# Spreading a block's row maxima one step later in the TensorE stream of an attention kernel

## The reference, cut to what matters

```python
x = _layernorm(x + _L0_attn_ref(x, Wq, Wk, Wv, Wo))
x = _layernorm(x + _L0_xattn_ref(x, ctx_768, ...))
x = _layernorm(x + _L0_ffn_ref(x, ...))

# cross-attention: 8 heads of 128, 1792 queries, 6000 keys
sim = jnp.einsum('hid,hjd->hij', qh, kh) * SCALE
mean = jnp.mean(sim, axis=-1, keepdims=True)
sim = (sim - mean) * ATTN_MATRIX_SCALE + mean
attn = jax.nn.softmax(sim, axis=-1)
out = jnp.einsum('hij,hjd->hid', attn, vh)
```

## Time and profile before

| what | before |
|---|---|
| median of 3 runs | 2277.97 us (2276.93 to 2280.52) |
| profiled execution | 2285.66 us, its span 2283.5 us |
| PE busy | 2233.7 us, 98% |
| DVE, ACT, POOL busy | 83%, 82%, 83% |
| granted TensorE clock | 0.996 over the span |
| chain that ended last | PE 76%, POOL 11%, DVE 5%, ACT 3%, DMA 3%, issue 2% |
| the 56 blocks | maxima reduced at 185.1 to 2152.7 us of the span |

### The profile page before, as it was taken

How to read it: one execution, slowest core, us unless ns; L and a number is a source line. 1 busy time by engine, 2 the same in 40 slices (tenths; PEclk the granted TensorE clock), 3 DMA queues, 4 the chain that set the end, 5 groups by cost and what they waited for, 6 DMA issues and landing times.

```text
span 2283.5 us, 61997 instructions
## 1 busy us (share of the span) xinstructions
PE 2233.7 (98%) x25966; PEld 1967.6 (86%) x25966; DVE 1891.8 (83%) x2111; ACT 1865.6 (82%) x2231; POOL 1899.2 (83%) x1157
## 2 busy tenths in 40 slices
PE   8999999999999999999999999999999999999998
PEld 4468998899889998999888997999889988988886
DVE  6878888888888888888888888888888888888877
ACT  5357888888888888888888888888888888888855
POOL 8865988888888897888888897888888888899853
PEclk9999999999999999999999999999999999999999
DMA  8310000000000000000000000000000000010320
GB/s 241 121 52 6 9 8 18 9 9 9 16 9 9 11 9 16 8 9 11 16 9 9 9 18 6 11 9 8 16 9 11 9 8 9 8 32 29 96 79 33
DMA packets 65302, 57.80 MB, mean 25 GB/s; under 512 B 32768, under 2 KB 57856, under 8 KB 65024
## 3 DMA queue, kind: packets, MB, share of 16 engines
q1 hardware_dynamic: 65024, 53.81, 8.3%
HBM read 30.99 MB, written 15.47 MB: 20 GB/s over the span
## 4 chain that ended last, share of the span: by engine, by line
PE 76%; POOL 11%; DVE 5%; ACT 3%; DMA 3%; issue 2%; SPq 0%; POOLq 0%; DVEq 0%; ACTq 0%
PE psum L460 30%; PE psum L492 10%; PE psum L485 10%; POOL e_lo L1720 7%; PE psum L488 5%; PE psum L490 5%; PE psum L625 4%; PE psum L615 4%; DVE run_max L1165 2%; POOL e_hi L1714 2%; ACT ring L917 2%; PE psum L763 2%; DMA fold_t<-run_max 1%; PE psum L632 1%; PE psum L811 1%
## 5 line engine op out<-in xcount | busy, mean ns | idle before, releaser
L1720 POOL TENSOR_TENSOR e_lo<-ring,e_hi 128x1024 f16<-128x1024 f32 (+1 forms) x665 | 1388.2, 2103 | 193.2 <-ACT ring L932 165.4
L917 ACT ACTIVATE ring<-psum 128x1024 f32<-128x1024 f32 (+1 forms) x672 | 674.5, 1004 | 169.4 <-POOL e_lo L1720 84.7
L1185 DVE SCALAR_TENSOR_TENSOR ring<-ring,psum 128x1024 f32<-128x1024 f32 (+1 forms) x672 | 793.0, 1187 | 0.4 <-PE psum L729 0.4
L1165 DVE TENSOR_TENSOR run_max<-psum,run_max 128x1024 f16<-128x1024 f32 (+1 forms) x560 | 670.2, 1197 | 146.0 <-ACT ring L917 142.3
L460 PE MATMUL psum<-qx_hi,k_hi 128*128 128x256 f16 x2632 | 718.4, 273 | 9.8 <-DVE run_max L1165 9.7
L460 PE MATMUL psum<-qx_hi,k_lo 128*128 128x256 f16 x2632 | 718.0, 273 | 0.0
L460 PE MATMUL psum<-qx_lo,k_hi 128*128 128x256 f16 x2632 | 717.9, 273 | 0.0
L492 PE MATMUL psum<-v_main,e_lo 128*128 128x129 f16 x4032 | 704.2, 220 | 0.0
L932 ACT ACTIVATE ring<-ring 128x1024 f32<-128x1024 f32 (+1 forms) x672 | 696.3, 1037 | 0.6
L485 PE MATMUL psum<-v_main,e_hi 128*128 128x257 f16 x2016 | 550.7, 273 | 1.6 <-POOL e_lo L1720 1.6
L488 PE MATMUL psum<-v_main,e_hi 128*128 128x129 f16 x2016 | 443.6, 220 | 0.0
(11 more groups left out here) (205 smaller groups left out, 3065.3 us busy)
## 6 DMA issues: line engine op xcount, KB each, us to landing
o_scratch<-o_buf SPq DMA_DIRECT2D x56, 128.0 KB, 1.9
raw<-o_scratch SPq DMA_DIRECT2D x14, 512.0 KB, 4.7
stage<-in_ctxT SPq DMA_DIRECT2D x6, 500.0 KB, 4.2
stage<-in_ctxT SPq DMA_DIRECT2D x12, 250.0 KB, 5.3
w_scratch<-wall SPq DMA_DIRECT2D x1, 2304.0 KB, 10.0
wall<-w_scratch SPq DMA_DIRECT2D x6, 384.0 KB, 3.2
x<-in_xT SPq DMA_DIRECT2D x4, 448.0 KB, 6.3
res<-in_x SPq DMA_DIRECT2D x1, 1792.0 KB, 15.8
```

The costliest lines, as they stand in the source:

```text
L917: a.activation(ring[:, f % SLOTS, 0:n], pair(f)[:, 0:n], ACT.Copy).then_inc(s_kept, 1)
L1165: v.tensor_tensor(run_max[:, 0:n], pair(f)[:, 0:n], before, ALU.max).then_inc(s_max, 1)
L1185: v.scalar_tensor_tensor(slot, slot, LIFT, psum[:, 6, 0:QB].unsqueeze(1).broadcast_to([P, t, QB]), ALU.add, ALU.subtract).then_inc(s_sub, 1)
L1720: g.tensor_tensor(e_lo[f % NEL][:, 0:n], slot, e_hi[f % NEH][:, 0:n], ALU.subtract).then_inc(s_lo, 1)
```

## The change

The call of `spread` moves within `step` of TensorE's stream. Before, it stood at step 8, behind the weighted values (`attend`) of that step. Now it stands at step 9, behind the scores of that step and ahead of that step's side product and weighted values. The functions, the waits and the other engines' streams stay as they are.

```diff
@@ -823,6 +823,8 @@
                         side(n, s, past, number)
                     if target < NBLK:
                         scores(n * NGRP + ahead, past, past * HEAD_SIDES, ts, target % 2)
+                    if s == MAX_S + 3 and -1 <= n < NBLK - 1:
+                        spread(n, n_at)
                     task = side_of(n, s)
                     if task is not None and not behind(n, s) and not ahead_of(n, s):
                         side(n, s, past, number)
@@ -833,8 +835,6 @@
                         attend(n * NGRP + s, past * NQB * NGRP, past * HEAD_SIDES)
                     if task is not None and behind(n, s):
                         side(n, s, past, number)
-                    if s == MAX_S + 2 and -1 <= n < NBLK - 1:
-                        spread(n, n_at)
                     turn = n * NGRP + s - TAIL
                     if turn in O_PROJECT:
                         o_project(*O_PROJECT[turn])
```

## The result

The changed kernel is slower: 2285.72 us, median of 8 runs (2283.73 to 2289.39), against 2278.26 us for the kernel before (8 runs, 2276.93 to 2280.52). The ratio is 1.0030, with a 95% interval of 1.0021 to 1.0039, so 4.8 to 8.9 us. The profiled execution took 2289.39 us, its span is 2287.3 us. The same pair, run again later beside each other, gave 1.0033 (1.0021 to 1.0045) for the changed kernel and 0.9994 (0.9985 to 1.0003) for an unchanged copy of the one before.

The account below looks back on a forecast made before the run. PE was taken to bound ordinary stretches, GpSimd those without value or key products. Terms 4.2 + 1.2 + 1.1 + 0 - 3.0 gave +3.5 us, raised to +5.5 for plain runs: 2277.97 + 5.5 = 2283.5 us, range 2275 to 2289.

Parts of the forecast that it names:

- What bounds it: PE sets ordinary stretches of 35.30 us; GpSimd and its boundary wait set those of 33.54 without value or key products.
- kind 2: Twelve blocks (n = 0, seven heads' fifth blocks, 50 to 53): PE waits at the spread, again before step 11's scores.
- term 3: Blocks 5 and 6 of five heads, PE and reduction arriving together: stall at step 10's key product, 1.1 us in all.
- The delay of 0.57 us: At n = 22, the next block's first subtraction starts at 1011.93, 0.57 us later: spread start plus 1.31, 0.28 and 0.04.
- The cover of 0.49 us: Before step 11's scores, 0.54 us after the running maximum, less the least distance 0.05: PE can absorb 0.49 us.
- Term 1: Eight GpSimd-bound stretches, from seven heads' fourth blocks and n = 49: seven pay 0.57 us whole, 4.0; 4.2 with n = 3.
- my own criterion: Forecast wrong if fourth-block stretches keep their length, predicted to grow from 33.56 to about 34.1 us between low parts.
- Terms 2, 3 and 4: Costs of 1.2 us in 15 blocks where PE reaches the spread last, 1.1 in `term 3`, nothing in `kind 2`.
- Term 2: Fifteen blocks, PE last at the spread: GpSimd's spare 1.8 us swallows the delay, 0.08 us left before step 11, 1.2 together.
- Term 5: Ten blocks with late maxima: PE does scores while waiting, gain 3.0 us, 0.6 kept at each of n = 19 and 33.
- From the profiled execution to the plain runs: Late maxima taken as a disturbance of the profiled execution, 7.7 us above the median; +3.5 us raised to +5.5 for plain runs.
- The sum with no late maxima: Without late maxima the whole kernel's loss was put at 4.6 + 1.8 + 1.4 = 7.8 us.

Follow-up runs that it names:

- only_waiting: Against the kernel before, the spread moved only in the 12 blocks where TensorE waited for it: 1.0001, 2279.29 us.
- copy_first_w: `only_waiting` with ScalarE's copy of the scores at step 9 put ahead of the waiting half exponential: 0.9954 against the kernel before, 2267.78 us.
- behind_attend: The spread moved one place further than in the changed kernel, behind the weighted values of step 9: 1.0378 against the kernel before, 2366.19 us.
- copy_first_a: The changed kernel with ScalarE's copy of the scores at step 9 put ahead of the waiting half exponential: 0.9926 against the kernel before, 2261.56 us.
- only_value: Against the kernel before, the spread moved only in a head's first three blocks (20 blocks, not n = 0 or the last head): 1.0012, 2281.78 us.
- again_after: The changed kernel, unedited, run again beside a copy of the kernel before: 1.0033, 2287.73 us.

## Why the prediction was right, and where it was not

The forecast was 2283.5 us, +5.5 over 2278; the first measurement is 2285.72, +7.5, the second +0.33% or about 7.5. Direction, range and the mechanism at each hand-off held; the step from the profiled execution to the plain runs did not. Step by step:

- **What bounds it.** Shown. The stall at the spread was not PE's loss in kind 2: taking it away in twelve blocks changed nothing (`only_waiting`), since the next wait there ends at the same time as before. `copy_first_w`, in which that next wait is gone too, gained nothing either, so behind both waits stands GpSimd. The earlier trace rows also left out a third wait that the change touches, that before key products, though term 3 counts it: it went from 3.8 to 8.6 us.
- **The delay of 0.57 us.** The composition held: spread plus 0.28 plus 0.04, seen again at 1014.87 and 1014.91. Measured from the reduction, though, the subtraction is only 0.08 later (2.60 us behind it for 2.52). VectorE's whole chain at the boundary, the reduction with it, now runs some 0.5 us later behind PE, so the delay shows in ScalarE's wait as 2.12 - 1.69 = 0.43 and not as 0.57. I had expected 2.3 there, and 2.6 for GpSimd's 2.37.
- **The cover of 0.49 us.** Held: 0.08 us per ordinary block predicted, 0.10 measured, and `behind_attend` shows the other side of the threshold. That what is queued behind the waiting exponential carries the stall is shown by `copy_first_a`.
- **Term 1, GpSimd's stretches:** 4.0 predicted for seven, 4.02 measured. But I named the wrong window for it. From low part to low part, as in the earlier trace rows, these stretches keep their length, for the delay comes in with their first instruction. On PE they are 0.55 to 0.59 longer. By my own criterion the term would have been called wrong; it was the criterion that was.
- **Terms 2, 3 and 4:** 1.49, 1.30 and 0.01 for 1.2, 1.1 and 0. In kind 2 the stall before step 11 grew from 0.39 to 0.90 us at n = 51, where I had 0.7, and PE's waits for `run_max` in all to 12.7 us in the first pair and 15.3 in the second, where I had 15 or more. Term 2's reason was too simple: `only_value` shows that part of a delay is carried into the following block.
- **Term 5, late maxima:** -2.8 predicted with n = 3, -2.55 and -1.37 measured. n = 19 and 33 keep 0.9 and 0.7 in the first pair, not 0.6.
- **From the profiled execution to the plain runs.** This step failed in its reason. I took the late maxima for a disturbance of the profiled execution, since that lay 7.7 us above the median. They return in every profile. The second profile of the same kernel is 7.0 us shorter: 4.0 of it lie ahead of the first block, 1.5 at n = 27, and only about 1.3 in blocks with late maxima. At the first two places the first profile has a lower granted clock (0.51 in the column PEclk, which is the level of 1.2 GHz where 1.00 is 2.4):

```profile
92.60:99.50 6.90, 6.12 (x24) 3.48 (x25) 5.31 (x11) 1.51 (x2) 2.55 (x3) 0.51 0.38 152
1202.00:1205.50 3.50, 3.50 (x20) 2.62 (x21) 0.46 (x1) 0.76 (x1) 1.62 (x1) 0.51 0.02 5
```

  The second profile has 1.00 in both. Three of the twelve profiles have the fall at 93 us; in them the scores of step 8 of n = -1 start at 183.3 to 183.9 us, in the nine others at 178.8 to 179.7. The sum with no late maxima had a slip besides: two more blocks at 0.25 make 1.6 of the 1.1, not 1.4, so 8.0 and not 7.8. The upward shift from 3.5 to 5.5 went the right way by luck.

Open is part of the rest: the parts read from the two pairs of profiles give 3.8 and 5.4 us, while plain runs differ by 7.5. Some of it goes with the granted clock, which is on record for every run of the experiments. Of 31 runs of the kernel before, the 14 with a mean clock of 1.000 took 2278.8 us on average, 11 with 0.999 took 2280.1, four with 0.998 took 2281.6 and two with 0.997 took 2285.3: some 2 us for each 0.001. In the second set the changed kernel's six runs have a mean of 0.9982. The sixteen runs of the kernel before beside them have 0.9989 and lie 7.5 us lower, the eleven of its copy have 0.9996 and lie 9.1 us lower. By my estimate the clock makes 1.4 and 2.8 us of these, which leaves some 6 of either, near the 5.4 of the profiles. Whether the change brings the lower clock or it fell so by chance, no run here shows. The profiled execution of `again_after`, 2284.03 us, is also the fastest of its six.

## What to carry to other kernels

A wait that is removed from the busiest engine is worth something only if the next wait on the same engine does not end at the same time as before; so follow the chain to the next place where two engines meet before counting the gain, and ask whether another engine sets the stretch all the same. A hand-off may be moved later by its cover for next to nothing (0.1 us a block here) and costs its full length beyond, where no other idle time is left; read the cover as the distance between the last needed result and its user, block kind by block kind, since one place in the code is several places in time. And where a late hand-off hurts, look at what stands behind the waiting instruction for no need of its own: moving one copy ahead of it gained 10.6 us by itself, and turned the studied change from 7 us of loss into 6.7 of gain. Before a profile that lies above the plain runs is given a cause, compare its granted clock with theirs. The best kernel of the study, `copy_first_a`, takes 2261.56 us, 0.74% less than before.

## What the runs showed of the hardware

A subtraction that waits for a matmul's result starts 0.04 us after the end that the profile gives the matmul (1014.87 to 1014.91, and in the earlier trace rows); in the changed kernel's profile it is 0.037 to 0.039 us in all 37 blocks where the subtraction waited. The Trainium skill says in "Perfetto Trace Analysis", section on the tensor engine instruction, that this end is estimated and that the time a semaphore takes to reach the other engine is in no record. No run here measures either; the distance of 0.04 us is then one between a model and a record, but it repeated and was good enough for terms of 0.1 us.

The lateness of a DMA transpose is tied to the place: 3.1 to 3.4 us of waiting at n = 19 in every profile, 1.67 in most others. No other DMA of the kernel's own is issued beside it, but a packet of queue 8, which the profile calls `instruction`, is. In the profile of the kernel before the queues are, from 897.7 to 900.8 us, while the transpose of n = 19 moves:

```profile
q1 hardware_dynamic: 544, 0.13, 22.2%
q8 instruction: 1, 0.02, 2.6%
```

Beside the transpose of n = 22, from 1006.8 to 1008.2 us, queue 8 has none. Over all twelve profiles 129 of 672 transposes landed more than 2.7 us after their issue, where 2.5 is usual. All 129 had a packet of queue 8 under way between issue and landing; of the 543 others 79 had. That such packets hold the transpose up is argued from this, not shown: no run moved one.

The granted clock fell at 18 places in the twelve profiles, the end of the span left out. Each time TensorE had just waited or was waiting, 1.96 to 2.81 us long; the fall came during the wait or at most 1.4 us after its end. At n = 27 of the kernel before it was this wait:

```profile
1201.97 0.39 PE L460 MATMUL psum<-qx_hi,k_hi 128*128 128x256 f16 x1 [2.49 <-DVE run_max L1165]
```

The copy of the same kernel waited 2.65 us at this place and kept 1.00; its stretch took 37.92 us, that with the fall 39.39.
